# Build of the adjacency panels: the operands of the loop's tile pairs move from fixed places to a ring of four pairs

## The reference

```python
m = ft[src] * w[:, None]
msum = jax.ops.segment_sum(m, dst, num_segments=n_nodes)
...
agg = jax.ops.segment_sum(x[row], col, num_segments=n)
```

## Time and profile before

| | |
|---|---|
| Time, median of 3 runs | 4106.24 us (4103.9 to 4116.88) |
| Profiled execution, its span | 4131.5 us |
| Build in it | from about 49 to 1108 us |
| PE, PEld, DVE, ACT, POOL busy | 3483.2, 2445.5, 1463.3, 1265.5, 871.1 us |

### The profile page before, as it was taken

How to read it: one execution, slowest core, us unless ns; L and a number is a source line. 1 busy time by engine, 2 the same in 40 slices (tenths; PEclk the granted TensorE clock), 3 DMA queues, 4 the chain that set the end, 5 groups by cost and what they waited for, 6 DMA issues and landing times. The chain is left out here.

```text
span 4131.5 us, 85615 instructions
## 1 busy us (share of the span) xinstructions
PE 3483.2 (84%) x23502; PEld 2445.5 (59%) x23503; DVE 1463.3 (35%) x4278; ACT 1265.5 (31%) x4012; POOL 871.1 (21%) x928
## 2 busy tenths in 40 slices
PE   5888889999988888968999999997777677776777
PEld 2345556777744434435999999985444445444545
DVE  6766667777601200024431111132222222222223
ACT  5566667878701300014322211232000000000001
POOL 2000000000010000000000000024666566666663
PEclk8999999999999999997999999997777778787778
DMA  2011222333495589861432222341222222222222
GB/s 60 1 46 62 69 70 87 106 101 119 133 231 127 136 188 230 196 169 31 124 107 78 76 77 77 89 115 48 65 63 63 60 63 63 62 63 63 61 63 55
DMA packets 120056, 381.79 MB, mean 92 GB/s; under 512 B 33166, under 2 KB 74620, under 8 KB 106026
## 3 DMA queue, kind: packets, MB, share of 16 engines
q1 hardware_dynamic: 90958, 324.81, 29.5%
q0 software_dynamic: 25664, 51.90, 5.7%
q10 hardware_dynamic: 3154, 1.60, 0.2%
HBM read 294.59 MB, written 83.62 MB: 92 GB/s over the span
## 5 line engine op out<-in xcount | busy, mean ns | idle before, releaser
L2266 POOL DMA_INDIRECT edge_rows<-src_table,src_idx x784 | 776.6, 991 | 471.2 <-issue 193.4
L685 ACT ACTIVATE build_scaled<-build_lanes,w 128x128 f32<-128x128 bf16 x1132 | 428.6, 405 | 307.4 <-DVE build_lanes L640 275.0
L756 PE MATMUL build_ps<-build_keys,build_scaled 128*128 128x300 bf16 (+1 forms) x2264 | 492.2, 299 | 20.5 <-ACT build_scaled L685 17.8
L640 DVE TENSOR_SCALAR build_lanes<-key_id,lane,one_w 128x128 f32<-128x128 f16 x1132 | 389.1, 344 | 237.9 <-PE build_ps L756 181.9
L2410 ACT ACTIVATE edge_act<-edge_ps 128x512 f32<-128x512 f32 x196 | 116.9, 597 | 1147.6 <-remote 741.7
L2382 PEld LDWEIGHTS edge_ps<-edge_hot,edge_act 128*128 128x128 f32 x1760 | 297.8, 244 | 263.5 <-issue 261.5
L1108 PE MATMUL prop_ps<-prop_rows,y 125*128 125x500 f32 (+1 forms) x1050 | 408.3, 546 | 50.0 <-DMA prop_rows<-adj_rows 43.2
L2360 PE MATMUL edge_ps<-m_store,edge_hot_t 125*128 x2640 | 269.1, 249 | 205.0 <-issue 126.0
L748 PE MATMUL build_ps<-build_keys,build_lanes 128*128 128x300 bf16 (+1 forms) x1132 | 345.3, 305 | 87.8 <-DVE build_keys L642 65.4
L642 DVE TENSOR_SCALAR build_keys<-key_id,key,win_base 128x300 bf16<-128x300 f16 (+1 forms) x1132 | 406.0, 359 | 0.5 <-issue 0.2
L2382 PE MATMUL edge_ps<-edge_hot,edge_act 128*128 x1760 | 316.3, 332 | 94.8 <-issue 58.9
(11 more groups left out here) (368 smaller groups left out, 4762.4 us busy)
## 6 DMA issues: line engine op xcount, KB each, us to landing
prop_rows<-adj_rows SPq DMA_DIRECT2D x85, 1367.2 KB
cnt_panels<-build_cnt SPq DMA_DIRECT2D x50, 683.6 KB
adj_rows<-build_adj_t SPq DMA_DIRECT2D x25, 1367.2 KB
n<-cnt_panels SPq DMA_DIRECT2D x40, 683.6 KB
orders_panel<-cnt_panels SPq DMA_DIRECT2D x40, 683.6 KB
edge_dst_row<-dst_rows SPq DMA_DIRECT2D x196, 125.0 KB
h<-cnt_panels SPq DMA_DIRECT2D x20, 683.6 KB
prop_rows<-adj_rows SPq DMA_DIRECT2D x85, 158.7 KB
```

The lines of the kernel that those rows point to most:

```text
L640: v.tensor_scalar(lanes[s][:], g.key_id[:, 0:128], g.lane[:, at], g.one_w3[:, at], ALU.is_equal, ALU.mult).then_inc(s_lanes[s], 1)
L685: a.activation(scaled[s][:], half(lanes[s], 1), ACT.Copy, scale=g.w12[:, bass.ds(t, 1)]).then_inc(s_scaled[s], 1)
L756: last = pe.matmul(ps[:, weight_bank(j), 0:KW[j % 2]], half(scaled[s], i), keys[s][:, 0:KW[j % 2]], start=False, stop=False, skip_group_ch ...
L2266: pool.indirect_dma_start(rows[s][:, i, :], None, dr.table, bass.IndirectOffsetOnAxis(ap=g.src_idx[:, t:t + 1], axis=0)).then_inc(s_rows[s ...
```

## The change

`lanes`, `scaled` and `keys` become four tiles each, held by a new class `Places`. Tiles 0 and 1 are the first tiles' places of even and odd windows, as before. Tiles 2 and 3 are for the first and the second tile of a pair and are four times as wide: a ring of four places, shared by the windows of both parities. There is one counter of pairs now in place of two, and the place is the counter's two low bits, taken by each engine in a register of its own. `s_free` of the two ring tiles starts at 4 in place of 1, so DVE and ACT may be up to four pairs ahead of PE. Every instruction of a pair's tile that reads or writes `lanes`, `scaled` or `keys` gets its address from a register; it was a constant. Arithmetic, order of matmuls, shapes and the number of tiles stay.

```diff
-        self.pairs = [Counter(eng) for side in range(2)]
+        self.pairs = Counter(eng)
...
-            n = self.pairs[j % 2].next()
+            n = self.pairs.next()
...
+class Places:
+    def __init__(self, ph, depth):
+        self.depth = depth
+        self.lanes = [ph.sb(f"lanes{i}", [128, 128 * (depth if i > 1 else 1)]) for i in range(4)]
+        self.scaled = [ph.sb(f"scaled{i}", [128, 128 * (depth if i > 1 else 1)]) for i in range(4)]
+        self.keys = [ph.sb(f"keys{i}", [128, KEVEN * (depth if i > 1 else 1)], BF16) for i in range(4)]
+
+    def of(self, eng, q, place, n):
+        i = q if place == 0 else 1 + place
+        at = None if place == 0 else eng.snap(n & (self.depth - 1))
+        return i, at
+
+    def wide(self, tile, at):
+        return tile[:] if at is None else tile[:, bass.ds(at * 128, 128)]
+
+    def narrow(self, tile, at, i):
+        both = tile[:].bitcast(BF16).rearrange("p (k two) -> p k two", two=2)
+        return both[:, :, i] if at is None else both[:, bass.ds(at * 128, 128), i]
+
+    def key(self, tile, at, width):
+        return tile[:, 0:width] if at is None else tile[:, bass.ds(at * KEVEN, width)]
...
-        SLOTS = 6
-        lanes = [ph.sb(f"lanes{s}", [128, 128]) for s in range(SLOTS)]
-        scaled = [ph.sb(f"scaled{s}", [128, 128]) for s in range(SLOTS)]
-        keys = [ph.sb(f"keys{s}", [128, KEVEN], BF16) for s in range(SLOTS)]
+        SLOTS, DEPTH = 4, 4
+        places = Places(ph, DEPTH)
...
-                    s = 3 * q + place
+                    s, r = places.of(v, q, place, n)
                     v.wait_ge(s_free[s], n)
-                    v.tensor_scalar(lanes[s][:], g.key_id[:, 0:128], g.lane[:, at], g.one_w3[:, at],
+                    v.tensor_scalar(places.wide(places.lanes[s], r), g.key_id[:, 0:128], g.lane[:, at], g.one_w3[:, at],
...
-                    a.activation(scaled[s][:], half(lanes[s], 1), ACT.Copy,
+                    a.activation(places.wide(places.scaled[s], r), places.narrow(places.lanes[s], r, 1), ACT.Copy,
...
-                    s, first = 3 * (j % 2) + place, place == 0
+                    (s, r), first = places.of(pe, j % 2, place, n), place == 0
+                    moving = places.key(places.keys[s], r, KW[j % 2])
                     pe.wait_ge(s_keys[s], n)
-                    done = pe.matmul(ps[:, count_bank(j, parity), 0:KW[j % 2]], half(lanes[s], 1), keys[s][:, 0:KW[j % 2]],
-                                     start=first, stop=False, skip_group_check=True)
+                    done = pe.matmul(ps[:, count_bank(j, parity), 0:KW[j % 2]], places.narrow(places.lanes[s], r, 1),
+                                     moving, start=first, stop=False, skip_group_check=True)
...
             for s in range(SLOTS):
-                pe.sem_inc(s_free[s], 1)
+                pe.sem_inc(s_free[s], DEPTH if s > 1 else 1)
```

More of the change, by code:

```diff
@@ L637, in tile @@
                     at = bass.ds(t, 1)
-                    s = 3 * q + place
+                    s, r = places.of(v, q, place, n)
                     v.wait_ge(s_free[s], n)
-                    v.tensor_scalar(lanes[s][:], g.key_id[:, 0:128], g.lane[:, at], g.one_w3[:, at],
+                    v.tensor_scalar(places.wide(places.lanes[s], r), g.key_id[:, 0:128], g.lane[:, at], g.one_w3[:, at],
                                     ALU.is_equal, ALU.mult).then_inc(s_lanes[s], 1)
-                    v.tensor_scalar(keys[s][:, 0:KW[q] + q], g.key_id[:, 0:KW[q] + q], g.key[:, at],
+                    v.tensor_scalar(places.key(places.keys[s], r, KW[q] + q), g.key_id[:, 0:KW[q] + q], g.key[:, at],
                                     g.win_base[:, q, bass.ds(e, 1)], ALU.subtract, ALU.is_equal).then_inc(s_keys[s], 1)
@@ L681, in tile @@
                 def tile(place, t, n):
-                    s = 3 * q + place
+                    s, r = places.of(a, q, place, n)
                     a.wait_ge(s_lanes[s], n)
                     a.wait_ge(s_free[s], n)
-                    a.activation(scaled[s][:], half(lanes[s], 1), ACT.Copy,
+                    a.activation(places.wide(places.scaled[s], r), places.narrow(places.lanes[s], r, 1), ACT.Copy,
                                  scale=g.w12[:, bass.ds(t, 1)]).then_inc(s_scaled[s], 1)
@@ L745, in tile @@
                 def tile(place, n):
-                    s, first = 3 * (j % 2) + place, place == 0
+                    (s, r), first = places.of(pe, j % 2, place, n), place == 0
+                    moving = places.key(places.keys[s], r, KW[j % 2])
                     pe.wait_ge(s_keys[s], n)
-                    done = pe.matmul(ps[:, count_bank(j, parity), 0:KW[j % 2]], half(lanes[s], 1), keys[s][:, 0:KW[j % 2]],
-                                     start=first, stop=False, skip_group_check=True)
+                    done = pe.matmul(ps[:, count_bank(j, parity), 0:KW[j % 2]], places.narrow(places.lanes[s], r, 1),
+                                     moving, start=first, stop=False, skip_group_check=True)
                     if first:
                         done.then_inc(s_opened, 1)
-                    pe.matmul(ps[:, weight_bank(j), 0:KW[j % 2]], half(lanes[s], 0), keys[s][:, 0:KW[j % 2]],
+                    pe.matmul(ps[:, weight_bank(j), 0:KW[j % 2]], places.narrow(places.lanes[s], r, 0), moving,
                               start=first, stop=False, skip_group_check=True)
@@ L755, in tile @@
                     for i in range(2):
-                        last = pe.matmul(ps[:, weight_bank(j), 0:KW[j % 2]], half(scaled[s], i),
-                                         keys[s][:, 0:KW[j % 2]], start=False, stop=False, skip_group_check=True)
+                        last = pe.matmul(ps[:, weight_bank(j), 0:KW[j % 2]], places.narrow(places.scaled[s], r, i),
+                                         moving, start=False, stop=False, skip_group_check=True)
                     last.then_inc(s_free[s], 1)
```

## The result

The changed kernel took 4056.97 us (median of 4 runs, 4055.92 to 4088.54) against 4105.07 us for the kernel before in the same session: a ratio of 0.9882, 95% interval 0.984 to 0.9924, or 48 us faster. The forecast was 4125 us, slower. The time lies in the range, the direction was wrong.

The account below looks back on a forecast made before the run. DVE and PE wait for each other in the build's loops; the ring replaces that by PE's sequencer at 1.90 us a pair. Stretches +22 - 12 + 9 = +19 us on 4106: 4125 us, range 4050 to 4190.

Parts of the forecast that it names:

- A tile: 0.30 + 3 x 0.13 = 0.70 us; a pair 1.40 us.: PE's sequencer in the build: 0.30 us of address operations ahead of a tile, then 0.13 us for each further matmul.
- The analogue at L2360: Edge-phase matmuls with register addresses, used as price model: one AND and five addresses in four matmuls, 0.30 us before the first.
- faster, by cheaper addresses: Rival: AND once a pair, one folded operation before each matmul, 0.48 us a tile; 4006 us, halfway 4073; chance 0.29.
- The turning point: Address price a tile, over 518 tiles of the first two stretches, at which the forecast's sign turns: 0.66 us.
- First stretch: Build's long loops, 9 windows with 76 pairs: 0.60 us a window, 1.90 a pair, 3 for the start; 153 us, +22.
- Second: Build's stretch of mostly loops of two, 78 windows with 183 pairs: 395 plus 13 us, 408 against 420, -12.
- the third stretch: Build's nearly all loops of one, 163 windows with 182 pairs: operations mostly hidden, 8 us for blocks and 1 for rest, +9.
- Hidden late: In the build's last stretch PE's sequencer leads the array by about 0.6 us, covering the 0.30 us ahead of a tile.
- the rival that charged 64 us there: Rival, slower because nothing hides late: 182 late pairs each show 0.35 us, 64 in place of 9; 4180 us; chance 0.15.
- DVE and ACT beside the path: Their address operations in the build, 0.12 us a tile on DVE, less on ACT, lie beside PE's work; on the path 106 us.
- the prediction's circle of DVE and PE: In the build DVE waits 181.9 us for PE to finish a tile, PE's loads 181.2 us for DVE's keys.
- The branch: PE's loop branch at L543: 215 ns taken, 67 not, part of 0.50 us a pair for the loop; the skill's 108 ns rejected.

Follow-up runs that it names:

- e2_pe_again: The changed kernel, but PE alone derives the place of a pair's second tile anew from a copy of the counter: 3934.73 us, ratio 1.0183 to the kernel before.
- e0_after: The changed kernel itself, run once more in another session: 4065.02 us against 4109.65 for the kernel before, ratio 0.9885.
- e3_dve_act_again: The changed kernel, but DVE and ACT, not PE, derive the second tile's place anew from a counter copy: 3838.85 us, ratio 0.993 to the kernel before.
- e4_depth2: The changed kernel with a ring of two pairs in place of four, same instructions: ratio 0.9883 to the kernel before.

## Why the prediction was wrong

**The step that failed: "A tile: 0.30 + 3 x 0.13 = 0.70 us; a pair 1.40 us."** It put the first tile's price on the second tile too. The first tile was right: its operations start at 70.8 us and the second tile's at 71.5. The second tile of the pair reuses the place and the products and has one operation a matmul: from 71.5 to 72.0, about 0.47 us. e2_pe_again put the second tile's AND and product back, with one copy, and the gain of 48 us became a loss of 68. A pair costs 1.16 and not 1.40 us of addresses, 1.65 and not 1.90 us with the loop. The analogue at L2360 had shown the reuse in its later matmuls, and I had named it in the rival "faster, by cheaper addresses", but had it as an AND made once a pair with everything folded, and gave it 0.29. The turning point that I had worked out, 0.66 us for a tile, was right in kind: the mean of the two tiles is 0.58.

**The rest of the sum holds with the right price.** First stretch: 9 x 0.60 + 77 x 1.65 + 3 = 135 us, measured 134.2. Second: 78 x 0.60 + 182 x 1.65 + 13 = 360, measured 362.7. Some of that closeness is luck: the 3 and the 13 us and half of the 0.60 were estimates that no run measured by themselves. Between the forecast of +19 us and the build's -52 lie 71 us. Of these, 259 pairs at 0.25 us are 65, and 8 are the third stretch, which grew by 1 us and not by 9.

**Hidden late.** The 182 late pairs got their 1.16 us each, and the stretch grew by 1.4 us, not by 9. The lead covers them; the rival that charged 64 us there is out at this price. The lead can be counted, from L543's ALU operation behind a pair to the start of that pair's last matmul: in the third stretch its median was 1.15 us before and is 0.44 now. So the operations took up more than half of it, and most of them did not show. The Trainium skill ("Advanced Engine Details and Errata", Engine Queue Depths) has 64 instructions in TensorE's queue. At that point of the loop at most 33 loads and matmuls were ahead of the array before and 25 in the changed kernel (e0_after), so these traces agree with it and don't measure it.

But the cover is thin. At 2.02 us a pair (e2_pe_again) the median lead is 0.14 us, and the same stretch grew by 28 us. Had the price of 0.70 been right, two thirds of e2_pe_again's +27, +63 and +28 us (0.25 of its 0.37 us a pair) would have come on top of the changed kernel: +20, -13 and +20 us on before, where the forecast had +22, -12 and +9 (an estimate). So the first two stretches were summed rightly from a wrong price, and the late one was undersized by some 10 us. How that divides between one-pair windows and the loops of two among them, I didn't measure.

**DVE and ACT beside the path**: right with the lead, by e3_dve_act_again. Without the lead they are on it, and the prediction's circle of DVE and PE had left ACT out.

**The branch.** It took 207 to 208 ns taken and 70 to 76 not taken, and the sums with 0.50 us for the loop fit within 3 us. The 108 ns of the Trainium skill ("Advanced Engine Details and Errata", Control Flow Timing) don't fit the taken one here; the measurement decides.

**What the prediction said would show it.** DVE's wait under 60 us: 56.0. Waits put down to "issue": yes. Second stretch shorter: yes; first longer: by 2 us. Some 12 register operations more a pair: 10. "Wrong it would be if a pair in the first window takes under 1.8 us": it took 1.65, and that was the sign.

## What to carry to other kernels

A ring addressed by a register trades a wait between engines for register operations on every engine that touches the ring. Price it on the slowest sequencer, operation by operation (here about 0.1 us each), and count what a second use in the same loop body can reuse: the first use pays the AND and the products, the next ones an addition. Two pairs of lead gave all of the gain. Where a loop body can be doubled so that the places are constants, the addresses and half of the branches go: here the pair then took 1.05 us in place of 1.65, and DVE set the pace.

## What the runs showed that I had not expected

- A circle of waits can run over an engine that the main wait does not name. PE's wait for ACT's scaled, 69.2 us before, made DVE's and ACT's address operations cost nearly as much as PE's in the long loops (0.27 and 0.30 us a pair by their parts, 0.40 together), and with a lead of two pairs DVE's and ACT's cost nothing that shows there.
- Three more register operations on PE in a loop body of 1.65 us cost 117 us of build over 441 pairs, 0.27 us a pair, of which the loops that were bound by the sequencer bore 0.35.
- The same program took 3866 us on one chip and 4106 on others, with a build that seems to be of the same length; the difference lay entirely behind it. The mean granted clock over the span was 0.952 to 0.954 in the profiles from the one and 0.912 to 0.918 from the others. From 2800 to 3800 us, in the edge phase, it was 0.88 to 0.91 in e4_depth2 and 0.77 to 0.81 in e0_after, while up to 2800 us the two were within 0.02 of each other. Whether the lower clock is the cause, or all of it, is not shown.
